# Decoder layer, cross-attention stage: pair reductions for the weight jobs' scales, a later norm, another order of ScalarE's evictions and of VectorE's range

## The reference, cut to what matters

```python
# cross attention, 16 heads of 16
q = split(x @ Wq + bq); k = split(ctx @ Wk + bk); v = split(ctx @ Wv + bv)
p = softmax(q @ k.T / 4, axis=-1)
x = layernorm(x + (p @ v) @ Wo + bo)          # eps 1e-5

def qgroup(w):                                 # groups of 128
    wmax, wmin = max(w), min(w)
    scales = clip(wmax - wmin, 1e-5, None) / 15
    base = clip(round(-wmin / scales), 0, 15)
    return (clip(round(w / scales) + base, 0, 15) - base) * scales
```

## Time and profile before

| | |
|---|---|
| median of 3 runs | 1294.68 us (1290.55 to 1294.69) |
| the profiled execution, its own time | 1292.86 us |
| its span, first to last instruction | 1291.1 us |
| mean granted TensorE clock | 0.886 |
| PE / PEld / DVE / ACT / POOL busy | 78 / 59 / 78 / 57 / 47 % |
| the cross stage, first to last clip | 345.2 to 581.9 us |

### The profile page before, as it was taken

The page is one execution under the profiler, slowest core; times in us unless marked ns, Lnnn a source line. Parts: engine busy times, 40 slices in busy tenths (PEclk is TensorE's granted clock), DMA queues, the critical chain, the costliest instruction groups (busy, mean ns, idle before and its releaser), DMA issues.

```text
span 1291.1 us, 25737 instructions
## 1 busy us (share of the span) xinstructions
PE 1005.1 (78%) x7366; PEld 756.9 (59%) x7367; DVE 1004.6 (78%) x2283; ACT 738.8 (57%) x1866; POOL 608.9 (47%) x805
## 2 busy tenths in 40 slices
PE   0334886772588898896799999983799999999980
PEld 0233332341477776774467767653688888888870
DVE  6894899999789888983788888856577777767755
ACT  4785644341488888882465555540566666666650
POOL 3896787776244444441255555543232332332225
PEclk9666978985789888986899999996899999999995
DMA  4953200002233333322123222230111111111105
GB/s 182 399 199 117 92 1 22 11 32 76 84 112 110 110 110 110 110 75 65 33 69 103 85 85 85 82 112 7 36 36 37 41 35 37 41 36 35 41 28 195
DMA packets 51884, 105.70 MB, mean 82 GB/s; under 512 B 9808, under 2 KB 36432, under 8 KB 51328
## 3 DMA queue, kind: packets, MB, share of 16 engines
q1 hardware_dynamic: 47472, 92.39, 20.8%
q0 software_dynamic: 4368, 12.78, 3.2%
HBM read 73.06 MB, written 32.10 MB: 81 GB/s over the span
## 4 chain that ended last, share of the span: by engine, by line
PE 48%; DVE 21%; issue 10%; POOL 6%; ACT 4%; DMA 1%; DVEq 0%; POOLq 0%; SPq 0%; ACTq 0%
PE banks L1996 14%; PE banks L2006 10%; PE banks L1360 4%; PE banks L1403 4%; DVE mix_sums L671 4%; PE banks L1382 2%; PE banks L1395 2%; POOL whole L1119 2%; PE banks L1352 2%; DVE carry L661 2%; ACT whole_level L1047 2%; DVE carry L658 2%; DVE whole_stat L227 2%; DVE peak L1150 1%; DVE top L642 1%
## 5 line engine op out<-in xcount | busy, mean ns | idle before, releaser
L2079 DVE SCALAR_TENSOR_TENSOR expert_gate<-banks,expert_steps,expert_chunk 128x128 f32<-128x128 f32 x546 | 166.1, 346 | 97.1 <-ACT expert_chunk L2041 92.7
L1996 PE MATMUL banks<-expert_parts,levels 128*128 128x128 bf16 x3276 | 228.8, 220 | 8.5 <-issue 5.6
L1996 PEld LDWEIGHTS banks<-expert_parts,levels 128*128 x3276 | 202.7, 98 | 49.2 <-issue 21.5
L2006 PE MATMUL banks<-down,up 128*128 x546 | 176.1, 406 | 0.0
L2041 ACT COPY expert_chunk<-banks 128x256 f32<-128x256 f32 x273 | 101.7, 372 | 102.4 <-PE banks L1996 87.9
L2134 POOL DMA_INDIRECT chosen_d<-expert_y,expert_target x39 | 39.1, 1001 | 203.5 <-ACT expert_y L2051 203.5
L519 PE MATMUL banks<-x_turned,w_rkv 128*128 128x512 f32 (+1 forms) x192 | 98.1, 670 | 38.8 <-DVE weight L652 38.3
L2045 ACT ACTIVATE silu<-expert_gate,expert_steps 128x128 f32<-128x128 f32 x273 | 110.7, 405 | 16.9 <-DVE expert_gate L2079 16.7
L414 PE MATMUL banks<-consts,level 128*128 128x128 f32 x154 | 35.6, 423 | 87.8 <-POOL level L397 87.8
L1119 POOL TENSOR_TENSOR whole<-whole_level,whole_stat 128x896 bf16<-128x896 f32 x32 | 53.3, 1686 | 102.4 <-DVE whole_level L1188 102.4
L2086 DVE SCALAR_TENSOR_TENSOR up<-expert_gate,expert_steps,silu 128x128 f32<-128x128 f32 x273 | 94.0, 344 | 9.3 <-ACT silu L2045 9.3
(11 more groups left out here) (237 smaller groups left out, 2512.7 us busy)
## 6 DMA issues: line engine op xcount, KB each, us to landing
whole_raw<-in_weight_jobs SPq DMA_DIRECT2D x16, 896.0 KB, 5.3
raw<-in_weight_jobs SPq DMA_DIRECT2D x11, 896.0 KB, 5.4
numbers_d<-turned SPq DMA_DIRECT2D x11, 896.0 KB, 5.0
levels_d<-whole_t SPq DMA_DIRECT2D x16, 448.0 KB, 2.7
levels<-levels_d SPq DMA_DIRECT2D x16, 448.0 KB, 3.8
down<-numbers_d SPq DMA_DIRECT2D x16, 448.0 KB, 4.4
finish_moe<-chosen_d SPq DMA_DIRECT2D x8, 512.0 KB, 7.5
normed_d<-normed_parts SPq DMA_DIRECT2D x16, 192.0 KB, 1.9
```

What stands on the lines that cost most here:

```text
L1996: last = pe.matmul(banks[:, at, (m * DC + c) * ROWS:(m * DC + c + 1) * ROWS], levels[:, bass.ds(expert * (2 * JOB) + (m * JOB + (f * DC + ...
L2006: last = pe.matmul(banks[:, Y + j, 0:D], up[j][:, f, :], down[:, bass.ds(expert * JOB + f * D, D)], start=(f == 0), stop=(f == FC - 1))
L2079: last = dve.scalar_tensor_tensor(out=gate[slot(j, f)][:, m, :], in0=halves(at)[:, m, 1, :], scalar=steps[j][:, m, 1, f:f + 1], in1=chunk[ ...
```

## The change

The diff, complete but for blank context:

```diff
-BIAS = LOW
+BIAS, NEG_MIN, SHIFT = LOW, MIN, HIGH
+
+def row_pair(a, m, o):
+    return a[:, m:o + 1:o - m, :].rearrange("p m (a b) -> p a b m", b=2)

 def group_range(dve, st, a, groups):
     dve.tensor_reduce(a[:, MAX, :], groups, AX.X, ALU.max)
-    st.did(dve.tensor_reduce(a[:, MIN, :], groups, AX.X, ALU.min))
+    st.did(dve.tensor_reduce(a[:, NEG_MIN, :], groups, AX.X, ALU.min, negate=True))

-def group_bias(dve, st, a):
+def group_bias(dve, st, a, spaced):
...
+    def in_pairs(m):
+        return a[:, m, :].rearrange("p (a b) -> p a b", b=2)
+    apart = spaced[:, :, 0:2]
     st.wait()
-    step(dve.tensor_tensor(a[:, TMP, :], a[:, MAX, :], a[:, MIN, :], ALU.subtract))
-    step(dve.tensor_scalar(a[:, SCALE, :], a[:, TMP, :], 1e-5, 1.0 / LEVELS, ALU.max, ALU.mult))
+    step(dve.tensor_reduce(apart, row_pair(a, MAX, NEG_MIN), AX.X, ALU.add))
+    step(dve.tensor_scalar(in_pairs(SCALE), apart, 1e-5, 1.0 / LEVELS, ALU.max, ALU.mult))
     step(dve.reciprocal(a[:, INV, :], a[:, SCALE, :]))
-    step(dve.scalar_tensor_tensor(out=a[:, TMP, :], in0=a[:, MIN, :], scalar=-1.0, in1=a[:, INV, :],
-                                  op0=ALU.mult, op1=ALU.mult))
-    step(dve.tensor_scalar(a[:, BASE, :], a[:, TMP, :], 0.0, LEVELS, ALU.max, ALU.min))
-    return dve.tensor_scalar(a[:, BIAS, :], a[:, BASE, :], MAGIC, None, ALU.add)
+    step(dve.tensor_reduce(apart, row_pair(a, NEG_MIN, INV), AX.X, ALU.mult))
+    step(dve.tensor_scalar(in_pairs(BASE), apart, 0.0, LEVELS, ALU.max, ALU.min))
+    return dve.tensor_reduce(in_pairs(BIAS), row_pair(a, BASE, SHIFT), AX.X, ALU.add)
...
+        spaced = k.buffer(own, "whole_spaced", [TILES // 2, 3])
...
             collect(0, n)
+            if more:
+                take_x(1 - j, n + 1)
             soften(1, n)
             if more:
-                take_x(1 - j, n + 1)
-            if more:
+                take_qk(1 - j, n + 1)
                 round_part(1 - j, n + 1, 0)
-                take_qk(1 - j, n + 1)
             tiles(0)
...
-        def join(j, n, i):
+        def join_stats(j, n):
...
+        def join_norm(j, n, i):
             dve.wait_ge(cross_scale, n + 1)
...
             if prev:
-                join(1 - j, n - 1, i)
-            if more:
-                take_values(1 - j, n + 1)
+                join_stats(1 - j, n - 1)
             if more == 2:
                 range_of(j, n + 2, i + 2 - j)
             if more:
+                take_values(1 - j, n + 1)
                 peaks(0, n + 1)
             normalise(j, n)
+            if prev:
+                join_norm(1 - j, n - 1, i)
...
         for j in range(2):
             dve.memset(v_ones[j][:, :, XK:XK + 1], 1.0)
+            st.did(dve.memset(stat[j][:, SHIFT, :], MAGIC))
...
-        join(1, B - 1, TURNS - 1)
+        join_stats(1, B - 1)
+        join_norm(1, B - 1, TURNS - 1)
```

More of the change, by code:

```diff
@@ L1183, in steps_of @@
                 dve.wait_ge(whole_ready, n - 1)
-            group_bias(dve, st, stat[j]).then_inc(scale_ready, 1)
+            group_bias(dve, st, stat[j], spaced).then_inc(scale_ready, 1)
         def clip(j, n):
```

## The result

| | before | after |
|---|---|---|
| median | 1293.34 us (4 runs) | 1276.44 us (4 runs, 1275.35 to 1280.66) |
| profiled execution | 1292.86 us | 1275.62 us |
| span | 1291.1 us | 1273.9 us |
| mean granted TensorE clock | 0.886 | 0.895 |
| first to last clip, 15 steps | 236.7 us | 220.7 us |

The ratio is 0.9888, 95% interval 0.9860 to 0.9916: 17 us, or 1.1%, faster, where 1290 us and a range down to 1279 were forecast. The 17.2 us between the two profiled executions are 16.0 in the fifteen steps of the stage and 3.7 in its tail (from the last clip to the last norm), with 0.4 gained before the stage and 2.9 lost behind it, where nothing was changed.

A forecast was written before the change was run, and what follows sets the result against it. VectorE, ScalarE and TensorE were all taken as near their limit, with ScalarE taking over once VectorE's waits go. 0.33 us over 14 steps, 4.6 us, off the median 1294.68 gave 1290 us, range 1279 to 1299.

The forecast's parts named there:

- port wait: VectorE's bias chain: the first subtraction's wait for GpSimd, 0.66 us a step on average, should go with pair reductions.
- VectorE's own saving: VectorE's list by itself: 15.78 - 0.66 - 1.06 + 0.05 = 14.1 us a step.
- part 4: ScalarE's new order: its loop rebuilt for each kind of step, changing them by -0.85, +0.1 and 0 us.
- three kinds: Cross-stage steps cut at the first softmax, by mean clock: 4 of 15.6 us, 5 of 15.4, 4 of 16.7.
- Fast step: Cross-stage step at clock 0.98 or 0.99: from 15.6 us to 14.75 by ScalarE's loop, put at 14.9.
- Middle step: Cross-stage step at clock 0.86 to 0.90: from 15.4 us to 15.5, with scores up to 0.3 us earlier.
- Slow step: Cross-stage step at clock 0.80 or 0.81: 16.7 us before and after.
- of this some 0.8 can go: Slow step: of TensorE's 1.69 us wait for VectorE before the second half's scores, some 0.8 us can go.
- The forecast's last sign: If the gain is over 15 us, TensorE's products were not what ScalarE waited for.
- The mix: Count of fast, middle and slow steps: from 4, 5, 4 to 6, 4, 3, making the gain 0.35 us a step.
- the clock stays up: Rival: VectorE's lead closes the gap before the second half's scores, all steps fast, 13 us gained, 1281; chance 0.25.
- The slower rival: Rival: keys first puts a 0.79 us pair of roundings on ScalarE's path, up to 7 us slower, 1302; chance 0.15.

The follow-up runs named there:

- before_act_plus: Kernel before with one more copy of 256 columns on ScalarE in each step, used by nothing: 1290.0 us, ratio 0.9977.
- before_filled: Kernel before with 12 unused TensorE products of 128 columns in front of the second half's scores: 1290.9 us, ratio 1.0010.
- act_order_alone: Kernel before with ScalarE's new order and nothing else: 1293.6 us, ratio 1.0025.
- pair_sums_alone: Kernel before with the pair reductions in the bias chain and nothing else: 1276.9 us, ratio 0.9900.
- u_late_norm: Changed kernel with the norm put back behind its statistics, all else kept: 1284.5 us, ratio 0.9928.
- x_first_only: Changed kernel with ScalarE's first two roundings ahead of keys and queries again, turned x still before the second softmax: 1272.3 us, ratio 0.9883.
- after_act_plus: Changed kernel with one more copy of 256 columns on ScalarE in each step, used by nothing: 1314.4 us, ratio 1.0163.
- best_act_plus: Changed kernel with x first, roundings ahead of the queries and early load, plus the extra 256-column ScalarE copy: 1273.6 us, ratio 0.9874.

## Why the prediction was wrong

**Right.** The port wait was sized at 0.66 us and left altogether; the norm went from 0.76 + 0.71 to 0.40 us; VectorE waited 0.33 us for the load; the two roundings stand behind the queries, with 0.46 us of idle time before the keys (482.21); nothing moved to the scale instruction. The sign and the order of VectorE's own saving (1.7 us a step) were right.

**The step that failed** is in part 4: "That is not the answer, because of part 4", with the reading under "What bounds" that "ScalarE closes the loop as tightly as VectorE does". before_act_plus shows that it did not: 0.4 us more on ScalarE left each kind of step as it was. A tail without a gap on an engine is no proof that the engine holds the loop. Its loop also has a head, from the first softmax to the query products, and that head was as long as it was because TensorE's scores started when VectorE released them (1.69 us of waiting in the slow step). The three kinds of step that the forecast built on were cut at ScalarE's softmax; cut at the clip, eleven of fifteen lengths are 15.73 to 15.79 us, and in such a step VectorE waits for no other engine but GpSimd (0.76 us). So a shorter list on VectorE shortened all kinds, where the forecast gave the middle and the slow kind nothing (+0.1 and 0).

**The terms that were mis-sized.** Fast step: 14.9 forecast, 14.25 measured. The query products end 5.17 us after the first softmax (481.12 + 1.06 - 477.01) where 5.54 was taken, and the tail is 7.25 us (484.00 to 491.25) where 7.40 was; the 0.15 added for VectorE's own end was not there. Middle step: 15.5 against 14.6. Slow step: 16.7 against 15.4. Here the term was "of this some 0.8 can go". The scores moved by 1.17 us (from 0.11 behind to 1.06 ahead of the softmax), and they moved out of the low clock, which took another 0.95 us off them (2.08 to 1.13). I had moved a duration without asking at which clock it would then run. The forecast's last sign, that a gain over 15 us would mean that ScalarE did not wait for TensorE's products, misled: the gain was 17 us, and ScalarE still waits for the queries (0.46 us before 482.21); they came earlier than forecast.

**The mix** was forecast to shift towards full clock; the stage's mean went from 0.89 to 0.92. But before_filled shows that the clock was no cause of its own in the kernel before. The rival "the clock stays up" came nearest to the outcome (1281), but not by its mechanism: the gap before the scores did close (0.21 us at 490.19), and yet nine of 14 steps still have a lower clock, and those that have not take 14.25 us and not 14.9.

**The tail** was left out of the sum. It runs from 15.1 to 20.7 us over these kernels, and its work is the same in all but for the twelve products of two of them and the time at which a norm is written; the stretch of the kernel before

```profile
581.90:601.70 19.80, 14.72 (x76) 12.05 (x74) 6.83 (x15) 7.10 (x13) 4.43 (x4) 0.64 0.24 80
```

had a clock of 0.64, the same code in before_act_plus

```profile
586.30:601.40 15.10, 11.12 (x76) 8.66 (x74) 6.91 (x15) 7.06 (x13) 4.43 (x4) 0.84 0.31 105
```

had 0.84 and took 4.7 us less. The tail's 3.7 us are therefore luck in where the clock fell, and the 2.9 us lost in later stages, where nothing was changed, are bad luck that nearly cancels it. In steps alone the change is worth 16.0 us, where the forecast had 4.6.

**The slower rival** was not what the change did, but its mechanism shows in the steps. The new order of ScalarE, keys first included, costs 4.1 us of steps on the kernel before (act_order_alone), and 3.7 us when one wait is left (pair_sums_alone 225.8 against u_late_norm 229.5, which differ in the orders of ScalarE and of the range alone). Two steps of u_late_norm, which repeat to the end of the stage:

```profile
516.14:530.94 14.80, 13.58 (x99) 10.93 (x98) 13.35 (x22) 12.94 (x31) 6.62 (x6) 0.92 0.35 120
530.94:546.86 15.92, 15.37 (x102) 11.64 (x98) 13.75 (x22) 12.95 (x32) 6.62 (x6) 0.86 0.34 112
```

Only with both waits gone does the new order gain its 2.1 us, and x_first_only points to the early x: with the roundings back in front of the queries another 1.9 us go. These are differences of single profiled executions, and the intervals of the ratios overlap; the early x was not run on the kernel before by itself. after_act_plus is where that rival would have been: 0.4 us of ScalarE away.

Why does either wait alone bring nearly all of the gain in total time? In steps it does not: 225.8 and 225.6 us against 220.7. The stages behind the cross stage, where nothing was changed, took 688.0 and 687.8 us in these two profiled executions and 692.3 in that of the changed kernel, and the tail another 1.0 us less. That hides the 5 us. Why the later stages differ stays open, and so does what each part of ScalarE's order is worth by itself. That the two instructions read from `whole_spaced` had to be laid out so was not tested either: no run has the pair sums without it.

## What to carry to other kernels

Before writing "another engine takes over at once", add half a microsecond to that engine in the kernel before, measure the step at more than one engine's instruction, and look for what starts the head of its loop: a gapless tail proves nothing if the head waits for someone else. An instruction that is long for its size hides a wait that no idle column shows, and another form of the same work (here a reduction over pairs in place of an instruction with two sources) can take it away: 173 ns against 837. When several engines are within a few per cent of each other, reorder for the waits that are left, and try the neighbours of a reordering: here the range's place did nothing that could be measured, and the version that takes back keys first and issues the load earlier is faster than the change.

## What the runs showed of the hardware that was not expected

The length of the step and the granted clock can repeat together: u_late_norm alternates 14.80 us at 0.92 and 15.92 at 0.86, the changed kernel ends on 14.26 at 1.00, 15.47 at 0.84 and 14.58 at 0.93, and after_act_plus has 17.03 to 17.16 at 0.80 in 13 steps. That each sets the other is a guess; no run changed one and held the other. Some 0.4 us of work on ScalarE, whose clock is not the one that falls, cost 2.4 us a step in one kernel (after_act_plus), 0.6 in another (best_act_plus) and nothing within a step in a third (before_act_plus). A scale instruction that reads seven pairs at a distance of three numbers and writes fourteen adjacent ones took 168 to 171 ns in 16 calls, the one in the middle of GpSimd's work included (480.61, while L1128 ran from 478.17 to 481.50). That agrees with the Trainium skill, "VectorE: DVE Perf Modes", Mode 2×_2P, if source and destination count as different there; which of their counts the engine compares, no run here shows.
